# Order of the scan slots: where TensorE, ScalarE and GpSimd put three steps of a slot

## The reference, cut to what matters

```python
scores = einsum('bqkgd,bskd->bkgqs', Qg, K) / scale      # causal
attn = softmax(scores, axis=-1)
out = einsum('bkgqs,bskd->bqkgd', attn, V)

def step(state, inp):                                     # over 512 time steps
    d, b, c, u = inp
    dA = exp(d[..., None] * A)                            # the decay
    state = state * dA + (d * u)[..., None] * b[:, None, :]
    y = einsum('bdn,bn->bd', state, c)                    # 16 states per channel
    return (state, y)
```

## Time and profile before

| | us |
|---|---|
| median of 3 runs (lowest to highest) | 1271.38 (1269.74 to 1272.44) |
| the profiled execution | 1268.8 |
| its span | 1267.1 |
| from the first to the last of the slots' reciprocals that VectorE runs every eight slots | 202.4 to 690.9 |
| VectorE busy in that stretch of 488.5 us | 451.71 |
| GpSimd, ScalarE, TensorE busy there | 442.07, 433.54, 411.47 |

### The profile page before, as it was taken

How to read it: one execution, slowest core, us unless ns; L and a number is a source line. 1 busy time by engine, 2 the same in 40 slices (tenths; PEclk the granted TensorE clock), 3 DMA queues, 4 the chain that set the end, 5 groups by cost and what they waited for, 6 DMA issues and landing times. The chain is left out here.

```text
span 1267.1 us, 18612 instructions
## 1 busy us (share of the span) xinstructions
PE 1079.4 (85%) x6368; PEld 643.5 (51%) x6368; DVE 805.8 (64%) x1195; ACT 670.0 (53%) x1440; POOL 672.2 (53%) x587
## 2 busy tenths in 40 slices
PE   7999748888888888888888995989999989999970
PEld 3444325555555555555555442444444446766740
DVE  5477689999999999999997466330580013233327
ACT  3566768888888888898887222201010112232220
POOL 1033379999999999999996700201040214445430
PEclk9999969999999999999999997989999999999995
DMA  6210001111111111122330302002107513344219
GB/s 199 85 35 18 18 18 34 35 35 34 34 35 34 35 30 31 34 51 76 101 84 9 134 34 100 34 27 73 67 2 243 170 35 121 127 129 129 77 53 371
DMA packets 51820, 94.74 MB, mean 75 GB/s; under 512 B 9806, under 2 KB 17998, under 8 KB 51728
## 3 DMA queue, kind: packets, MB, share of 16 engines
q1 hardware_dynamic: 44208, 72.82, 18.1%
q0 software_dynamic: 7520, 20.72, 5.3%
HBM read 74.51 MB, written 20.84 MB: 75 GB/s over the span
## 5 line engine op out<-in xcount | busy, mean ns | idle before, releaser
L604 POOL TENSOR_TENSOR w_all<-w_all 128x512 f32<-128x512 f32 x256 | 320.4, 1270 | 0.7 <-POOLq L96 0.3
L778 DVE TENSOR_TENSOR_SCAN w_all<-da,w_all 128x512 f32<-128x512 f32 x256 | 297.8, 1205 | 0.0
L712 ACT ACTIVATE da<-w_all,a_flat 128x512 f32<-128x512 f32 x256 | 179.4, 701 | 9.0 <-PEq L96 7.7
L683 PE MATMUL yb<-ident,w_all 128*128 128x128 f32 x1024 | 161.6, 281 | 7.5 <-DVE acc L786 7.5
L633 PE MATMUL sc<-w_all,attn 32*128 32x384 f32 (+3 forms) x512 | 105.0, 486 | 45.3 <-ACT w_all L720 22.8
L720 ACT ACTIVATE w_all<-sc,neg_max 128x128 f32<-128x128 f32 (+3 forms) x256 | 133.9, 539 | 16.6 <-DVE neg_max L770 15.6
L659 PE MATMUL ob<-w_all,v 128*32 128x128 f32 x1280 | 94.7, 277 | 52.6 <-ACT w_all L729 52.6
L1166 POOL TENSOR_TENSOR w_all<-w_all 128x512 f32<-128x512 f32 x24 | 29.1, 1212 | 195.0 <-ACT w_all L1335 195.0
L683 PEld LDWEIGHTS yb<-ident,w_all 128*128 128x128 f32 x1024 | 113.6, 141 | 37.0 <-issue 30.7
L770 DVE TENSOR_REDUCE neg_max<-sc 128x2 f32<-128x256 f32 (+3 forms) x128 | 104.1, 813 | 34.0 <-PE sc L636 34.0
L1227 PE MATMUL pc<-w_all 128*128 128x512 f32 x256 | 114.3, 603 | 12.9 <-DVE w_all L1375 12.9
(11 more groups left out here) (199 smaller groups left out, 1635.2 us busy)
## 6 DMA issues: line engine op xcount, KB each, us to landing
w_all<-b_scratch SPq DMA_DIRECT2D x64, 256.0 KB, 3.3
w_all<-in_w_up SPq DMA_DIRECT2D x16, 512.0 KB, 6.1
w_all<-in_w_down SPq DMA_DIRECT2D x16, 512.0 KB, 7.0
w_all<-sorted_y SPq DMA_DIRECT2D x16, 512.0 KB, 10.6
attn<-in_x SPq DMA_DIRECT2D x4, 1024.0 KB, 7.2
w_all<-in_x SPq DMA_DIRECT2D x16, 256.0 KB, 4.1
norms<-attn SPq DMA_DIRECT2D x4, 1024.0 KB, 4.3
out_dram<-acc SPq DMA_DIRECT2D x16, 256.0 KB, 8.3
```

The costliest lines, as they stand in the source:

```text
L604: pool.tensor_tensor(dbu[:, k, :], keep["du"][i // N][:, k * T:(k + 1) * T], b_all[i % 2][:, :], ALU.mult).then_inc(pool_dbu.sem, pool_dbu ...
L683: last = pe.transpose(yb[which][:, k * P:(k + 1) * P], state[i % 2][:, k, t * P:(t + 1) * P], ident[:, :])
L712: act.activation(da[unit % 2][:, :], keep["dt"][i // N][:, k * T:(k + 1) * T], ACT.Exp, scale=keep["a_flat"][:, unit % (N * KD):unit % (N ...
L778: dve.tensor_tensor_scan(state[i % 2][:, k, :], da[unit % 2][:, :], dbu[:, k, :], 0.0, ALU.mult, ALU.add).then_inc(dve_scan.sem, dve_scan. ...
```

## The change

Four moves, no instruction is added or removed. On GpSimd the add runs behind both products of the slot. On TensorE the first group of turn_state runs first in the slot; in a spread slot the spread follows it; weigh_v comes behind these. On ScalarE the first decay of the slot follows the exponentials directly, ahead of the first copy (or the spread's copy), and the second decay follows weigh_c, ahead of the second copy (and ahead of the late first copy of a spread slot).

```diff
@@ gpsimd @@
                 if g + 1 < UNITS:
                     weigh(2 * g + 2)
+                    weigh(2 * g + 3)
                 if 0 <= g - 3 < UNITS:
                     add(g - 3)
-                if g + 1 < UNITS:
-                    weigh(2 * g + 3)
@@ tensor @@
             for g in range(UNITS + 3):
+                if 0 <= g - 2 < UNITS:
+                    turn_state(g - 2, 0)
+                if spread_in(g) is not None:
+                    spread(spread_in(g))
                 if 0 <= g - 3 < UNITS:
                     weigh_v(g - 3)
                 if 0 <= g - 2 < UNITS:
-                    turn_state(g - 2, 0)
-                    if spread_in(g) is not None:
-                        spread(spread_in(g))
-                    else:
+                    if spread_in(g) is None:
                         turn_prob(g - 2, 0)
                     turn_state(g - 2, 1)
-                elif spread_in(g) is not None:
-                    spread(spread_in(g))
@@ scalar @@
                     exponent(g, 1)
+                if g + 1 < UNITS:
+                    decay(2 * g + 2)
                 if spread_in(g) is not None:
                     spread(spread_in(g))
                 elif 0 <= g - 2 < UNITS:
                     turned(g - 2, 0)
-                if g + 1 < UNITS:
-                    decay(2 * g + 2)
                 if 0 <= g - 2 < UNITS:
                     weigh_c(g - 2)
+                if g + 1 < UNITS:
+                    decay(2 * g + 3)
+                if 0 <= g - 2 < UNITS:
                     if spread_in(g) is not None:
                         turned(g - 2, 0)
                     if (g - 2) % NT >= 2:
                         turned(g - 2, 1)
-                if g + 1 < UNITS:
-                    decay(2 * g + 3)
```

## The result

The changed kernel takes 1292.91 us (median of 4 runs, 1291.4 to 1295.19) where the kernel before takes 1271.53: a ratio of 1.0171, interval 1.0149 to 1.0193. It is slower by about 21 us; the forecast was a gain of 11. The profiled execution spans 1289.7 us, against 1267.1.

A forecast was written before the change was run, and what follows sets the result against it. The pace was set by the chain copy, weigh_v, turn_state, scores, maximum, with VectorE nearly full. Per octet +0.30, -0.79, +0.20, -0.43 make -0.72 us; 15 octets -10.8, first octet -0.3: 1271.38-11.1 = 1260.3 us, range 1252 to 1274.

The forecast's parts named there:

- TensorE's move: Slots 1 and 2: turn_state 0 fills the wait for ScalarE's copy, saving 0.43 us, or 0.79 in the spread slot.
- The 0.43 us taken for slot 1: Slot 1: the chain behind the copy's end is shorter by 0.50-0.06 = 0.44 us, taken as 0.43.
- ScalarE's move: Second copy of slot 1 late by nothing; of slot 0 by 0.61 us, making slot 1 longer by 0.20 and 0.30.
- The gap of a change of shape: Spread slot: with spread and weigh_v side by side, one weight-load gap goes, 0.20 us (between 0 and 0.3).
- Rival 1: Slots 1 and 2: copy late in both, +1.22 us an octet, 1278.9 us in all; chance 0.18.
- GpSimd's move: GpSimd's slots: second product earlier, add later by 1.24 us; cost 0, gain 0, as no pace-setting engine waits for it.
- I count 0: Slots 0 and 3: TensorE's queue behind weigh_c fits VectorE's time, 3.07 against 3.13 us in slot 0, so no cost.
- The cover of 0.06 us: Slot 0: room left for TensorE's queue; links dearer by 0.05 each would add 0.2 us twice an octet.
- the chance of 0.17 for slower: Whole kernel: chance that the change makes it slower by more than about 0.2% (2.5 us).

The follow-up runs named there:

- both idle stretches filled: The changed kernel, order untouched, with slot 3's four transposes of turn_state 1 and the score matmuls behind them made twice; 1261.87 us, ratio 0.9938.
- the mixed order: The changed kernel with weigh_v ahead of turn_state in slots 0 and 3, and ScalarE's second decay of slot 0 behind the second copy, as before; 1256.77 us, ratio 0.9911.

## Why the prediction was wrong

**Slots 1 and 2, TensorE's move: right.** Slots of 4.05, 4.85 and about 4.3 us were forecast; they measured 4.05, 5.04 and 4.28 where the clock was high, in the changed kernel and in all fours of the one with both idle stretches filled. The wait in front of weigh_v fell to 0.25 to 0.3 us. The 0.43 us taken for slot 1 came out only beside ScalarE's move (4.49 us with ScalarE's order alone, 4.05 with both); TensorE's order alone gave nothing there.

**The gap of a change of shape: mis-sized.** I took 0.20 us off the spread slot for spread and weigh_v standing side by side. It lasts 5.04, not 4.85. From the spread's start to that of the next group it is now 0.91 us (416.39 to 417.30) instead of 1.01 (407.56 to 408.57), so half of the gap went. Before:

```profile
408.57 0.66 PE L683 MATMUL yb<-ident,w_all 128*128 128x128 f32 x4
```

The other half of the error is the spread's start, 0.14 us behind the copy's end (415.65 + 0.60 to 416.39) where weigh_v starts some 0.05 behind it:

```profile
415.65 0.60 ACT L727 ACTIVATE w_all<-tb 128x512 f32<-128x512 f32 x1
```

```profile
416.39 1.08 PE L669 MATMUL tb<-ident,rinv 128*32 128x128 f32 x32 [0.34 <-ACT w_all L727]
417.30 1.04 PE L658 MATMUL ob<-w_all,v 128*32 128x128 f32 x16
418.28 0.66 PE L682 MATMUL yb<-ident,w_all 128*128 128x128 f32 x4
```

Beside this row the Trainium skill's rule (TensorEngine Tiling (Array Packing), Key Properties: a change of mode drains TensorE) holds in direction: spread and weigh_v side by side are closer by 0.10 us, where I took 0.20.

**ScalarE's move: right in both places.** In slot 1 the second copy is late by nothing (it starts at 415.65, as turn_prob's end of 415.62 lets it), in slot 0 the decay is paid: +0.20 in the half without and +0.30 in the half with the spread. ScalarE's order alone confirms both: slot 1 +0.64 to +0.74, slot 2 unchanged. Rival 1 as I had it, a late copy in slot 2 too, did not happen.

**GpSimd's move: right.** Alone it measures nothing. Its waits turned into waits for a scan, as forecast: 60.9 us of them, and nobody waits for it.

**Slot 0: the step that failed.** "I count 0": the queue behind VectorE's weigh_c, 3.07 us against a cover of 3.13. Its length was right (slot 0 is 3.19 at full clock). What I priced nowhere was what the wait itself does. Moving weigh_v behind it turned TensorE's 0.23 us of idleness in front of turn_state into 0.79, next to the 0.99 for the exponentials that was there already, or to 0.66 where it was 0.23 (slot 3's order did that: in the mixed order, with the old one in slot 3, it is 0.23 again). Behind such pairs the clock halves in 19 of 30 fours. The cover of 0.06 us, named as the weak point, was all there was for a queue whose instructions take half as long again and more. I had read the granted clock of the slots as a fact (1.00) and not as something that the order of TensorE's work keeps up. Without the clock an octet is 32.02 us (the slots of the run with both idle stretches filled), a gain of 8 us in all; with the changed order untouched and the clock held up, 1261.87 us was measured, beside a forecast of 1260.3 for the changed kernel. That the two times are so near is in part luck: the sum was a gain of 11, this run's gain is 8, and the kernel before took 1.5 us less beside it. The octets are 30.7 us longer in the changed kernel than there, and that is the clock.

This case's rows say it first, the pair of waits in a stage where TensorE is busy for nearly nine tenths. The Trainium skill (TensorE: Matmul & The Clock Gate, "A second HAM failure mode: psum-queue depth-cycling") speaks of TensorE idling briefly and often between groups of matmuls until its clock swings between the two levels; the trace agrees, with waits of 0.66 and 0.79 us and then 0.54 over 3.7 us.

The range of 1252 to 1274 and the chance of 0.17 for slower both rested on late copies and a long queue. Neither had a case in which instructions become slower.

**Left open.** Why the clock is spared in 11 of 30 fours, and stays low into slot 1 in 5, isn't settled. Ten of the 11 have the shorter pair, but 5 fours with that same pair are slow: at 252.66 us TensorE waits 0.66 and at 254.16 us 0.79, and the transposes behind take 0.63 us, where the seam shown above has 1.09. Nor is it settled why the pair of 0.99 and 0.79 us brings 7 falls in one kernel and 14 or 15 in two others. That slot 2 gives 0.14 us back in the mixed order wasn't tried apart.

## What to carry to other kernels

Before moving work behind a wait on TensorE, ask what idle stretch it used to fill, and add up TensorE's idleness over neighbouring waits; the total over a stage says nothing (here it fell by 14 us while the kernel lost 21). Where the granted clock is 1.00, treat it as kept up by the order of the work: a chain with little cover is to be priced at half the clock as well. And an order written once for all slots is a compromise: the same move won 0.4 to 0.6 us in slot 2 and lost 1.4 in slot 0 wherever the clock fell.

## What the runs showed of the hardware

- TensorE's granted clock was 0.54 over 3.7 us in a stage where TensorE is busy 87% of the time (447.12 of 511.40 us), with no wait above 1.0 us in it. The fall came behind a pair of waits with 0.7 us of work between them: in 14 of 15 fours behind 0.99 and 0.79 us and in 5 of 15 behind 0.66 and 0.79. It came in none of 15 behind 0.23 and 0.79, 0.66 and 0.57, or 0.55 and 0.57.
- Useless matmuls that shortened the first wait by 0.44 us and the second by 0.22 turned a loss of 21 us against the kernel before into a gain of 8 (1292.91 and 1261.87 us).
- A single wait of 1.02 us in every slot 1 was followed by no fall there (clock 0.99; its 2 falls lie at the seams).
